# Four moves of small work in an attention and mixture-of-experts kernel: weight chunks, centroid split, slot release, gates

## The reference

```python
# x: (16, 256, 128), ctx: (16, 64, 128), 16 heads of 8, 8 experts, 2 shared experts, F = 512
q, k, v = (einsum('bsd,ed->bse', ., W)  split into heads)          # Wq, Wk, Wv
scores = einsum('bhqd,bhkd->bhqk', q, k) / sqrt(8)
attn   = softmax(scores, axis=1)                                     # over heads
x = x + einsum('bsd,ed->bse', attn @ v, Wo)                        # q from layernorm(x), k, v from ctx
...
y = layernorm(x)
raw = einsum('bsd,ed->bse', y, centroids)
_, top_idx = top_k(sigmoid(raw + routing_bias), 2)
top_w = softmax(take_along_axis(sigmoid(raw), top_idx))
shared_out = sum over n of gelu(y @ Wfc_sh[n].T) @ Wproj_sh[n].T
routed_out = sum over the two chosen e of top_w * gelu(y @ Wfc_r[e].T) @ Wproj_r[e].T
x = x + y + shared_out + routed_out
```

## Time and profile before

| | us |
|---|---|
| median of 3 runs | 389.18 |
| lowest and highest run | 387.49, 391.11 |
| the profiled execution, whole | 387.26 |
| its span from first to last instruction | 385.5 |
| TensorE busy | 331.7 (86%) |
| VectorE busy | 274.6 (71%) |
| ScalarE busy | 263.7 (68%) |
| GpSimd busy | 260.3 (68%) |

### The profile page before, as it was taken

One profiled execution on the slowest core, in us unless ns is written; L12 is line 12 of the kernel. 1 busy time (PEld: TensorE's weight loads), 2 busy tenths in 40 slices (PEclk: granted clock), 3 DMA queues, 4 the chain that ended last, 5 costly groups with the idle time before them and its releaser, 6 DMA issues.

```text
span 385.5 us, 11809 instructions
## 1 busy us (share of the span) xinstructions
PE 331.7 (86%) x4100; PEld 272.6 (71%) x4101; DVE 274.6 (71%) x592; ACT 263.7 (68%) x498; POOL 260.3 (68%) x268
## 2 busy tenths in 40 slices
PE   4777687598989879999999898899999999999253
PEld 1563365476777668888887676798998989999253
DVE  3879999997989969906756446677676776776246
ACT  2886999478696747574536787576776667767746
POOL 6354698789998682777777773077777777777600
PEclk9996999789999999999999999999999999999858
DMA  7956344310000000111114611323243232331098
GB/s 251 342 158 265 102 129 130 100 40 3 2 4 2 2 2 7 51 57 48 56 50 125 100 54 49 91 67 87 66 108 93 67 87 75 81 94 49 2 352 304
DMA packets 29179, 36.16 MB, mean 94 GB/s; under 512 B 4932, under 2 KB 24007, under 8 KB 28624
## 3 DMA queue, kind: packets, MB, share of 16 engines
q1 hardware_dynamic: 24592, 27.13, 23.5%
q0 software_dynamic: 4544, 8.44, 7.0%
HBM read 21.74 MB, written 14.72 MB: 95 GB/s over the span
## 4 chain that ended last, share of the span: by engine, by line
PE 34%; issue 18%; DVE 18%; POOL 16%; DMA 6%; ACT 6%; POOLq 1%; SPq 1%; DVEq 0%; ACTq 0%
POOL results L518 7%; PE banks L1499 5%; DVE Mx L929 4%; POOL gathered L500 4%; DVE Z L943 3%; POOL E L446 3%; ACT E L642 2%; PE banks L1483 2%; PE banks L1599 2%; PE banks L1484 2%; PE banks L1485 2%; PE banks L1601 2%; PE banks L1585 2%; PE banks L1603 2%; PE banks L1586 2%
## 5 line engine op out<-in xcount | busy, mean ns | idle before, releaser
L518 POOL DMA_INDIRECT results<-E,qRep x78 | 86.1, 1104 | 42.3 <-issue 27.4
L500 POOL DMA_INDIRECT gathered<-xs,slot x64 | 64.7, 1011 | 25.7 <-issue 18.3
L1224 DVE TENSOR_TENSOR E<-hid,E 128x512 f16<-128x512 f32 x78 | 54.0, 692 | 36.3 <-ACT E L783 36.3
L446 POOL TENSOR_TENSOR E<-E,rZ 128x1024 f32<-128x1024 f32 x32 | 67.6, 2133 | 13.4 <-DVE rZ L946 13.3
L781 ACT ACTIVATE hid<-banks 128x512 f32<-128x512 f32 x78 | 47.0, 602 | 38.2 <-DVE E L1224 22.6
L1599 PE MATMUL banks<-wprojL,E 128*128 x312 | 54.6, 219 | 2.9 <-DVE E L1224 1.9
L1603 PE MATMUL banks<-wprojH,E 128*128 x312 | 54.3, 219 | 0.0
L1601 PE MATMUL banks<-wprojH,E 128*128 x312 | 54.2, 219 | 0.0
L783 ACT ACTIVATE E<-banks 128x512 f16<-128x512 f32 x78 | 47.3, 606 | 0.0
L642 ACT ACTIVATE E<-banks 128x1024 f32<-128x1024 f32 x32 | 33.1, 1090 | 18.6 <-PE banks L1356 18.6
L1585 PE MATMUL banks<-qRep,wfcH 128*128 128x256 f16 x156 | 42.6, 273 | 0.9 <-ACT E L783 0.5
(11 more groups left out here) (227 smaller groups left out, 868.5 us busy)
## 6 DMA issues: line engine op xcount, KB each, us to landing
qRep<-gathered SPq DMA_DIRECT2D x39, 129.0 KB, 2.2
qRep<-q_rows SPq DMA_DIRECT2D x32, 128.0 KB, 2.5
qRep<-results SPq DMA_DIRECT2D x8, 512.0 KB, 7.4
X<-in_x SPq DMA_DIRECT2D x4, 512.0 KB, 6.3
q_rows<-qRep SPq DMA_DIRECT2D x8, 256.0 KB, 2.1
out<-X SPq DMA_DIRECT2D x8, 256.0 KB, 3.2
results<-E,qRep POOLq DMA_INDIRECT x78
gathered<-spare SPq DMA_DIRECT2D x9, 129.0 KB, 4.4
```

The lines of the kernel that those rows point to most:

```text
L446: g.tensor_tensor(heads, heads, rZ[:, k % 2, :].unsqueeze(1).unsqueeze(3).broadcast_to([P, HH // 2, P, 2]), ALU.mult).then_inc(attn_ready, 1)
L500: g.indirect_dma_start(out=gathered, out_offset=bass.IndirectOffsetOnAxis(ap=slot[:, k, i:i + 1], axis=0), in_=xs[:, i, :], in_offset=None ...
L518: g.indirect_dma_start(out=results, out_offset=bass.IndirectOffsetOnAxis(ap=xg[:, k, h, 2 * D:ROW].bitcast(I32), axis=0), in_=yg[:, k, h, ...
L1224: v.tensor_tensor(gL[:, j, 2 * c:2 * c + 2], hid[:, 2 * j + c].rearrange("p (c q) -> p c q", c=2), gH[:, j, 2 * c:2 * c + 2], ALU.subtract ...
```

## The change

- Weight chunks: the list for units 5, 6 and 7 is one, one and two chunks before; it is two, two and none now.
- `split_centroids` stands ahead of the first group of units on VectorE, not behind unit 1's maximum.
- `place` releases GpSimd (`slot_ready`) behind the first choice's slots, ahead of the second choice's. The token numbers that the release had waited for are written in `scores_in`.
- The gates' work on VectorE, eight instructions, stands ahead of the whole making of the tile table, not in its middle and behind it. Their exponential on ScalarE goes from pass 14 to pass 9 of the shared experts, ahead of its last chunk.

```diff
-WEIGHT_UNITS = ((), ((3, 0),), ((3, 1),), ((3, 2),), ((3, 3),), ((4, 0),), ((4, 1),), ((4, 2), (4, 3)))
+WEIGHT_UNITS = ((), ((3, 0),), ((3, 1),), ((3, 2),), ((3, 3),), ((4, 0), (4, 1)), ((4, 2), (4, 3)), ())
...
-            for i in range(8, HALVES):
-                gelus(i, i % 2, True)
+            gelus(8, 0, True)
+            for c in range(FC):
+                if c == FC - 1:
+                    act.wait_ge(rneed, 6)
+                    s.activation(r1[:, 4:6], r1[:, 4:6], ACT.Exp).then_inc(rexp, 1)
+                gelu(9, 1, c, True)
...
-                if i == SHARED * PAIRS - 2:
-                    act.wait_ge(rneed, 6)
-                    s.activation(r1[:, 4:6], r1[:, 4:6], ACT.Exp).then_inc(rexp, 1)
                 half_gelus(i, i % 2, i == HALVES)
...
-                    if first and k == 1:
-                        split_centroids()
...
+            split_centroids()
             four_units(0, True, False)
...
+                v.tensor_copy(xs[:, t, 2 * D:ROW].bitcast(I32), token[:, 0, t].unsqueeze(2))
...
-                    then(v.tensor_copy(slot[:, k, t], r1[:, 9, t]))
-                v.tensor_copy(xs[:, t, 2 * D:ROW].bitcast(I32), token[:, 0, t].unsqueeze(2)).then_inc(slot_ready, 1)
+                    last = v.tensor_copy(slot[:, k, t], r1[:, 9, t])
+                    if k == 0:
+                        last.then_inc(slot_ready, 1)
+                    else:
+                        then(last)
...
             dve.wait_ge(slot_ready, 2)
+            then(v.reciprocal(rt[:, 3], rt[:, 1]))
+            for n, hot in enumerate((6, 9)):
+                then(v.tensor_tensor(rt[:, 5], rt[:, hot], rt[:, 3], ALU.mult))
+                then(v.tensor_reduce(r1[:, 4 + n], rt[:, 5], AX_X, ALU.add))
+            then(v.tensor_tensor(r1[:, 6], r1[:, 4], r1[:, 5], ALU.max))
+            v.tensor_tensor(r1[:, 4], r1[:, 4], r1[:, 6], ALU.subtract).then_inc(rneed, 1)
+            v.tensor_tensor(r1[:, 5], r1[:, 5], r1[:, 6], ALU.subtract).then_inc(rneed, 1)
```

More of the change, by code:

```diff
@@ L1166, in _ @@
             ej, sj, rj = (tj[:, i * MAX_TILES:(i + 1) * MAX_TILES] for i in range(3))
-            then(v.reciprocal(rt[:, 3], rt[:, 1]))
-            for n, hot in enumerate((6, 9)):
-                then(v.tensor_tensor(rt[:, 5], rt[:, hot], rt[:, 3], ALU.mult))
-                then(v.tensor_reduce(r1[:, 4 + n], rt[:, 5], AX_X, ALU.add))
             then(v.tensor_tensor(passed, tile_no[:], end.unsqueeze(1).broadcast_to(wide), ALU.is_ge))
@@ L1182, in _ @@
             v.tensor_scalar(table[:, 0, 0:MAX_TILES], ej, float(EXPERTS - 1), None, ALU.min).then_inc(table_ready, 1)
-            then(v.tensor_tensor(r1[:, 6], r1[:, 4], r1[:, 5], ALU.max))
-            v.tensor_tensor(r1[:, 4], r1[:, 4], r1[:, 6], ALU.subtract).then_inc(rneed, 1)
-            v.tensor_tensor(r1[:, 5], r1[:, 5], r1[:, 6], ALU.subtract).then_inc(rneed, 1)
             for e in range(SHARED):
```

## The result

The changed kernel took 386.78 us, the median of 16 runs (385.33 to 388.57), where the kernel before took 389.50 on the same chip (16 runs). The ratio is 0.9929 [0.9909, 0.9950], 2.8 us less. A second set of runs gave 0.9945 [0.9919, 0.9972], 2.1 us less (1.4 by the medians alone). The forecast was 3.1 us less. Ratios compare fast executions of both kernels; for the last four experiments they don't follow the medians, because most executions of the kernel before on that chip count as slow.

The account below looks back on a forecast made before the run. Bound by the attention's ring of engines, then TensorE, fully busy from 152 to 205, and a two-branch join ahead of the routed tiles: 1.3 + 1.8 = 3.1 us less than the median 389.18, so 386.1 us, range 383.6 to 389.4.

Parts of the forecast that it names:

- The attention: Centroid and weight chunk moves together shorten the attention by 1.3 us, bounds 0 and 2.9, taken near GpSimd's 1.14.
- The steps on GpSimd: Chunk moves add 1.15 us and remove 2.29 on GpSimd, so unit 8's normalising starts at 93.6, not 94.73.
- The bound of 1.06: Most that unit 2's maximum can come forward: started at 40.74, its raw scores there at 39.68; 0.8 taken.
- The join: Where VectorE's shared add and the scatters meet ahead of the routed stage: 1.8 us gained, bounds 0.9 and 1.8.
- The later of them gives 239.6: Routed stage opens when TensorE's branch is ready, 239.6, the scatters' rows being there at 239.15: 1.8 us gained.
- What is late next is again VectorE's add, by 0.4 us over the scatters: After the change VectorE's last shared add, not the scatters, still decides the routed stage's opening, by 0.4 us.
- So the whole train comes 1.17 us forward: Releasing the first choice's slots at once moves all 64 GpSimd scatters 1.17 us earlier.
- ScalarE decides: Rival: unit 8's exponentials move 2.9 us in the attention, 4.7 us in all, time 384.5; chance 0.14.
- The slow case: Rival: VectorE's quarter 2 copy waits for the whole padding burst, holding TensorE; 5.0 us slower, 394.2; chance 0.07.
- Table loads dearer: Rival: ScalarE's moved table loads each cost twice their share in expert pass 9; sum 1.8, 387.4; chance 0.06.
- The attention gives nothing: Rival: unit 7's values, 1.15 us late on GpSimd, hold TensorE; only 1.8 us gained, 387.4; chance 0.17.
- The scatters don't move: Rival: GpSimd's early release fails, held by something else; join 0.9, sum 2.2, 387.0; chance 0.08.

Follow-up runs that it names:

- the last four experiments: Two kernels with added matmuls and two with one attention edit each, on another chip where the kernel before took 472.51 us; only their attention is used.
- e1: Kernel before with the two attention edits alone, weight chunks and centroid split: 386.82 us, ratio 0.9973.
- e5: The changed kernel itself, timed again against the kernel before: 386.98 us, ratio 0.9945.
- e7: Changed kernel with SyncE's nine padding writes held back until VectorE has made most late low halves: 386.59 us, ratio 0.9957.
- e11: Kernel before with the centroid split's move alone, on the slow chip: 471.07 us, ratio 1.0105.
- e12: Kernel before with the weight chunks' move alone, on the slow chip: 472.35 us, ratio 1.0077.
- e8: Changed kernel with VectorE's two additions put ahead of the two low halves behind the slots: 385.34 us, ratio 0.9899.
- e2: Kernel before with early slot release and gates' moves, without the attention edits: 388.65 us, ratio 0.9994.
- e3: Kernel before with the early slot release alone: 388.62 us, ratio 1.0006.
- e4: Kernel before with the gates' moves alone, on VectorE and ScalarE: 388.72 us, ratio 1.0008.

## Why the prediction came out right

**The attention: its total held, its reason did not.** Forecast 1.3 us; e1 measured 1.0 (0 to 2.1), and its trace, e5's and e7's are 1.35 to 1.4 shorter. The steps on GpSimd came out where the clock was full. Counted from unit 0's exponentials, the Newton steps start at 47.5 in e1 and e5 (before 47.60; forecast "when they did"), and unit 8's normalising at 63.0 (before 64.23; forecast 1.14 earlier). But e11, which has the centroids alone, comes to the same place, 62.8. GpSimd of e1 and of e11 at unit 8:

```profile
93.45 4.24 POOL L446 TENSOR_TENSOR E<-E,rZ 128x1024 f32<-128x1024 f32 x2
```

```profile
92.92 4.23 POOL L446 TENSOR_TENSOR E<-E,rZ 128x1024 f32<-128x1024 f32 x2
```

So the chunks' move costs in unit 5 what it gives back behind unit 7: in e12 unit 8's normalising stands 51.0 us behind unit 2's exponentials, before 50.9. What the prediction put down to the chunks is the centroids' gain, which reached all of the ring and which it sized at 0.8, of at most 1.06. They give 1.0 to 1.3 up to unit 2. The bound of 1.06 stood on unit 2's raw scores at 39.68, and those moved forward too; the pair also costs 0.3 us in its new place, not 1.45, because GpSimd has nothing under way there. That the wrong share and the wrong bound add up to 1.3 is luck.

**The join: mis-sized, 1.8 against 0 to 0.4.** The failed step is "The later of them gives 239.6". TensorE's branch went as forecast: both waits are gone, and no table load holds it. "What is late next is again VectorE's add, by 0.4 us over the scatters" did not hold: the scatters' branch is late, by 2.0 to 2.9 us of TensorE's idle time. "So the whole train comes 1.17 us forward" holds for its start (1.16) and not for its end, where the longer scatters had given all of it back, so the routed rows came when they had. The rest of that term was right: the step from SyncE's first load to the first transpose, forecast as 2.2, was 2.2 to 2.4 in seven kernels (2.9 in e5 and 3.7 in e8). That leaves 1.0 us at the first transpose, and the range named this end, "Bounds: 0.9". What the prediction has no term for is the price of the new wait: the clock fell behind it, and by the fourth tile 0 to 0.4 us are left. The median of e2 (0.2, at most 1.2) agrees.

**The sum came out in part by luck.** 1.35 for the attention and 0 to 0.4 for the join make 1.4 to 1.8, less than the 2.8 and 2.1 that were measured (intervals 1.9 to 3.5 and 1.1 to 3.1), so the forecast was met although more than half of it, the join, is hardly there. Where the rest comes from is open; e1 and e2, timed apart, add up to 1.2 (0.9967), less than e5's 2.1 but inside its interval. Part of it may lie behind the fourth tile, where no edit is: from there to the end it is 137.3 to 137.7 us in before, e2, e3 and e4, and 136.3 to 136.7 in five of the six kernels with the attention edits (137.2 in e7). And every distance is held against a single execution of the kernel before, one of its fastest.

**The rivals.** *ScalarE decides* did not come: unit 8's exponentials waited 2.31 us for TensorE in the changed kernel, and 0.66 in e1 and e5, where the clock hadn't fallen. *The slow case* had its wait, 4.1 to 5.5 us at quarter 2's copy in e2, e4 and all from the changed kernel, and TensorE had none behind it; in the changed kernel the copy began at 207.92, and TensorE came to its first split chunk at 211.02. (The forecast's "at 207.9" is a coincidence: the scatter started later than forecast and landed in 3.3 us, not 6.28.) In e7 the wait stayed without the padding, so the burst isn't its cause. *Table loads dearer* failed: 2.86 us for both. *The attention gives nothing* looked true in the profiled execution (100.56), and was the clock's doing: in e5, the same kernel, it is 98.71. *The scatters don't move* (join 0.9, sum 2.2) is what the join did up to the first tile, though not for its reason: the release works, and the length of what it released takes it back. Of the times measured, one lies nearer to this rival and one nearer to the forecast, so only the traces tell them apart.

**What the forecast had no row for.** The last sentence named TensorE's lower clock in units 6 to 8. It came in the changed kernel at 82 to 86 and in e8, not in e5; it costs 1 to 1.5 us there and 1.6 at 144. It is no part of the change's effect as far as the runs tell (the mean clock of the timed runs is much the same, median 0.963 for the kernel before, 0.958 and 0.962 for the changed kernel), but makes a single profiled execution worth ±1.5 us.

## What to carry to other kernels

Where two branches meet, work out the ready time of both from the same view before promising the gain of one, down to the consumer's own start; the second branch's margin caps it. Then measure at a point where the consumer keeps its steady step again (here the fourth tile), since a longer wait can slow what comes right behind it. Before two profiled executions are compared, hold each one's time against the median of its kernel, and its granted clock by stage against the other's: here that decides the sign. A hole on the bottleneck engine that is too short to name (a pair of 8-column instructions that ended only with GpSimd's) was worth more than 2.3 us of work moved on an engine that looked full, to a unit in which that engine was full too.

## What the runs showed of the hardware

- An indirect DMA's instruction on GpSimd has no fixed length: 0.97 us for most of the 64 scatters, and up to 1.5 if it starts inside a VectorE instruction on 128x512 whose operands all lie in SBUF. It then ends 0.83 to 0.86 us behind that instruction (106 of 122 such scatters), 1.03 behind it if it is the first of the train (nine). Reading a PSUM bank, VectorE's instruction of the same size lengthened none of 23. The Trainium skill ("SBUF — State Buffer", SBUF: two separate sides) describes a lock on a port pair that VectorE and GpSimd share, which keeps GpSimd from writing descriptors during certain VectorE instructions; that would fit, but no run here shows the lock itself.
- Behind a wait of 2.0 to 2.9 us at the join TensorE's clock fell to 1.2 GHz for 3.4 us in eight of nine kernels (not in e4, which waited 2.70), and the first tiles took 0.5 to 1.1 us longer; behind the 0.90 us of the kernel before it did not.
- Two VectorE instructions on 128x8, a cast and a subtraction, took 0.14 and 0.17 us ahead of unit 0, with GpSimd idle. Behind unit 1's maximum, beside GpSimd's subtractions on 128x512, they took 0.42 to 0.65 and about 1.07, and each ended 0.02 to 0.03 us behind one of GpSimd's (six kernels). So small work on VectorE can cost as much as what GpSimd has under way.
- 30 small matmuls of TensorE in idle stretches made the kernel 2.2 us faster and its runs more alike (1.4 us apart against 3.4); the mean granted clock of its runs rose from 0.962 to 0.974.
- One chip ran the same kernel 21% longer, 472.5 against 389, with instructions of the same duration and idle gaps between them from 150 us on; not explained.
